# A graph attention kernel: in the last layer the row products are dealt to other engines

## The reference

```python
h = (x @ W.T).reshape(n, H, D)
alpha = einsum(h[src], a_src) + einsum(h[dst], a_dst)
enc = relu(edge_attr @ edge_W.T + edge_b).reshape(-1, H, D)
alpha = leaky_relu(alpha + sum(enc * h[dst], -1), 0.2)
ex = exp(alpha - segment_max(alpha, dst)[dst])
attn = ex / maximum(segment_sum(ex, dst)[dst], 1e-10)
out = segment_sum(h[src] * attn[..., None], dst) + bias
x = layernorm(x + out)
```

## Time and profile before

| | |
|---|---|
| median of 3 runs | 2146.94 us (2145.23 to 2147.84) |
| the profiled execution | 2150.75 us, span 2148.9 us, granted clock 0.844 |
| busy in the span | PE 1676.9 us (78%), DVE 1659.5 (77%), POOL 1552.5 (72%), ACT 1071.4 (50%) |
| row products on ACT, all layers (L1414) | 1840 instructions, 511.3 us |
| row products on POOL, the last layer (L1237) | 200 instructions, 129.0 us |

### The profile page before, as it was taken

How to read it: one execution, slowest core, us unless ns; L and a number is a source line. 1 busy time by engine, 2 the same in 40 slices (tenths; PEclk the granted TensorE clock), 3 DMA queues, 4 the chain that set the end, 5 groups by cost and what they waited for, 6 DMA issues and landing times. The chain is left out here.

```text
span 2148.9 us, 42137 instructions
## 1 busy us (share of the span) xinstructions
PE 1676.9 (78%) x9240; PEld 1039.6 (48%) x9240; DVE 1659.5 (77%) x4633; ACT 1071.4 (50%) x3670; POOL 1552.5 (72%) x1714
## 2 busy tenths in 40 slices
PE   7387888888885667778777776578999999899884
PEld 5244544544453434445444444345555555555551
DVE  5578877777779546666666667868999999999988
ACT  3134443443342435445455553546666666666655
POOL 3767777777777377777777776567778877778763
PEclk9578777877876868887888887879999999999985
DMA  6754444455640244444444641243444444444421
GB/s 195 178 144 134 140 139 137 138 140 155 185 124 29 89 127 136 135 135 134 134 130 135 198 121 37 91 124 106 130 135 132 127 125 129 132 130 134 133 67 60
DMA packets 131322, 274.32 MB, mean 128 GB/s; under 512 B 40389, under 2 KB 65968, under 8 KB 131061
## 3 DMA queue, kind: packets, MB, share of 16 engines
q0 software_dynamic: 64128, 181.33, 30.5%
q1 hardware_dynamic: 62259, 86.45, 13.4%
q10 hardware_dynamic: 4699, 3.86, 0.6%
HBM read 255.34 MB, written 17.20 MB: 127 GB/s over the span
## 5 line engine op out<-in xcount | busy, mean ns | idle before, releaser
L1225 POOL DMA_INDIRECT rows<-table,index_all x1320 | 1284.2, 973 | 481.1 <-issue 344.0
L1658 PE MATMUL bank<-rows,onehot 128*128 128x264 f32 (+1 forms) x2640 | 984.7, 483 | 178.1 <-ACT rows L1414 91.1
L826 DVE TENSOR_TENSOR sums<-sums,bank 128x264 f32 (+1 forms) x1320 | 552.7, 419 | 202.5 <-PE bank L1658 106.1
L1658 PEld LDWEIGHTS bank<-rows,onehot 128*128 128x128 f32 x2640 | 498.4, 224 | 386.7 <-ACT rows L1414 153.1
L1414 ACT ACTIVATE rows<-rows,wgt 128x33 f32<-128x33 f32 (+2 forms) x1840 | 511.3, 358 | 0.1
L1366 ACT CAST onehot<-bank 128x768 f32<-128x768 bf16 x240 | 177.7, 742 | 197.6 <-PE bank L1581 193.9
L1422 ACT ACTIVATE prod<-bank 128x512 f32<-128x512 f32 x240 | 134.8, 562 | 205.7 <-PE bank L1670 185.4
L815 DVE TENSOR_TENSOR rows<-rows,wgt 128x260 f32<-128x260 f32 (+2 forms) x480 | 216.0, 450 | 0.7 <-ACT wgt L1407 0.6
L1677 PE MATMUL bank<-late,onehotT 128*128 x1320 | 193.9, 283 | 0.7 <-DVE prod L835 0.7
L1373 ACT COPY scoreT<-bank 44x256 f32<-44x256 f32 (+2 forms) x120 | 39.5, 329 | 274.4 <-PE bank L1611 224.0
L835 DVE TENSOR_TENSOR prod<-prod,bank 128x512 f32<-128x512 f32 x240 | 151.8, 632 | 11.5 <-PE bank L1677 6.9
(11 more groups left out here) (200 smaller groups left out, 1787.6 us busy)
## 6 DMA issues: line engine op xcount, KB each, us to landing
locb<-loc_d SPq DMA_DIRECT2D x120, 352.0 KB, 3.8
rows<-table,index_all POOLq DMA_INDIRECT x1320
flags<-flags_d SPq DMA_DIRECT2D x520, 27.5 KB
table<-rows SPq DMA_DIRECT2D x25, 136.0 KB, 1.9
table<-rows SPq DMA_DIRECT2D x25, 134.0 KB, 3.0
late<-table SPq DMA_DIRECT2D x1, 3300.0 KB
table<-rows SPq DMA_DIRECT2D x25, 129.5 KB, 2.0
late<-table SPq DMA_DIRECT2D x1, 3212.5 KB, 14.8
```

Of the source, the lines that this page charges most:

```text
L826: done(v.tensor_tensor(a, a, sum_bank(l, t, s)[:, 0:VV], ALU.add), "add")
L1225: g.indirect_dma_start(out=rows[:, t.u, s, 0:ROW[l]], out_offset=None, in_=table[l], in_offset=bass.IndirectOffsetOnAxis(ap=index_all[:, t ...
L1658: done(m.matmul(sum_bank(l, t, s)[:, 0:VV], onehot[:, t.u, s, :], rows[:, t.u, s, 0:VV], start=True, stop=True), "agg")
```

## The change

One string: the word of the last layer in `OWNER`.

```diff
-OWNER = ("VAVVAVAVVVV", "VAAAAAAAAAA", "VVAVPAPPAPP")
+OWNER = ("VAVVAVAVVVV", "VAAAAAAAAAA", "VVVAPAPAPAP")
```

## The result

| | before | after |
|---|---|---|
| median, fastest to slowest | 2147.39 us (2145.23 to 2149.95, 4 runs) | 2176.78 us (2175.35 to 2177.55, 4 runs) |
| span of the profiled execution | 2148.9 us | 2175.2 us |
| DVE busy | 1659.5 us (77%) | 1652.9 us (76%) |
| ACT busy | 1071.4 us (50%) | 1124.5 us (52%) |
| POOL busy | 1552.5 us (72%) | 1533.2 us (70%) |

The kernel is slower by 29 us: ratio 1.0131, interval 1.0118 to 1.0145. The forecast was 2152, with a range to 2160. The direction was right and the size was not.

The account below looks back on a forecast made before the run. It took DVE alone to bound from row 4's add to the rescale, PE from there to row 4's add. 36 x (0.06 + 0.08) = +5.0 us on 2150.75 gave 2155.8; less 3.8 for the median, 2152, range 2149 to 2157.

Parts of the forecast that it names:

- two signs of being wrong: Row 4's product under 5.3 us after the rescale would mean faster; L717 waiting over 0.1 us would mean slower.
- The loop over row 0, row 2's load and row 4: Rescale, row 0's add, PE rows 2 to 4, row 4's add, DVE's own work: 17.00 us; change adds 0.06 a batch.
- The 0.58 us that DVE gains ahead of that wait: Dot product after row 0's add starts 0.58 us earlier; the gain ends at row 4's add, which waits for PE.
- DVE's product behind the rescale: Row 2's product, placed between rescale and row 0's add, takes 0.43 us against 0.71 for row 3's product now.
- The 11 us of this rule alone: VectorE and GpSimd exclusion alone would save 0.3 us a batch, 36 x -0.3 = -11 us, giving 2136.
- ACT's chain: On ACT, row 7's product, copy and exponentials precede step 6's encoding, whose end moves from 1723.74 to 1724.82.
- ACT becomes the pacemaker: Slower rival: ACT's chain 0.3 us longer than summed delays dot product and L717; +16 us, 2163; chance 0.08.
- PE's 1.06 us at row 8: PE's largest wait, for ACT at row 8, disappears; a rival had it on the path: -38 us, 2109, chance 0.02.
- Cost: +0.08 us a batch, with no slack behind it: DVE's dot product (L835) can start at 1724.86 instead of 1724.78, waiting for ACT's encoding; bounds 0 and +0.28.
- Row 7's add on DVE comes only behind the dot product of 1724.72, which takes 0.68, so the new wait is covered: PE's row 7 product comes about 0.6 us later, at 1724.4, but costs DVE nothing at row 7's add.
- From that add to the next rescale, 10.83 us, DVE stands for nobody else: From row 4's add to the rescale, DVE alone sets the pace, waiting for no other engine.
- The 0.06 of slots 2 and 3: Row 2's product behind the rescale delays row 0's add and row 4's add by 0.06 us a batch; bounds 0.00, +0.4.

Follow-up runs that it names:

- the best version: Kernel before with DVE on slots 0 and 2, ACT 1, 3, 5, 8, POOL the rest, register load at step 3: 2138.46 us against 2149.26, ratio 0.9949.

## Why the prediction was wrong in its size

The direction was right, for a reason that the forecast had: the encoding does come too late. But at a chance of 0.44 for slower against 0.41 for the same it was not sure of it, and five sixths of the loss come from something that its sum doesn't hold. Neither of its two signs of being wrong showed: row 4's product did not start earlier than 5.3 us after the rescale, and L717 did not wait.

Right, by its own steps:

- **The loop over row 0, row 2's load and row 4.** Row 0's add at +0.68 (forecast 0.68), row 2's load at +1.22 (1.23), row 4's product at +5.41 (5.42), the wait at row 4's add 0.49 (0.5). The 0.58 us that DVE gains ahead of that wait bought nothing. Slots 2 and 3 alone cost +2.8 us (0.6 to 4.9) where 2.2 were forecast.
- **DVE's product behind the rescale** took 0.42 us and not 0.71. The Trainium skill ("SBUF — State Buffer", Who interferes with whom) has VectorE and GpSimd shut each other out here; the trace agrees that the product is short once no product of POOL lies beside it (POOL's first one starts at 1712.13, and this product ended at 1711.28). The 11 us of this rule alone weren't gained, as the saving lies ahead of a wait.
- **ACT's chain.** Encoding at +9.42 and its end at +10.00, where the five steps summed to +9.44 and +10.04. The rival "ACT becomes the pacemaker", priced at 0.3 us more of chain, falls with this. Its 2163 was the nearest of the cases to the result, by luck: its chain isn't longer than summed.
- **PE's 1.06 us at row 8** are gone and bought nothing.

Wrong: the step "Cost: +0.08 us a batch, with no slack behind it", and the bounds on it, 0 and +0.28. The dot product is indeed 0.09 us late. But I priced a late instruction at its own lateness, and put the register load at nothing, without a word on it. The wait took something from the sequencer besides: its lead. What stood behind the dot product in DVE's order was not only row 7's add but also the load of 1.29 us, and all but 0.27 us of it (0.87 against the 0.60 without a load) had been hidden by that lead. The term is 0.09 + 0.73 = 0.82 us a batch where 0.06 + 0.08 = 0.14 was summed: 36 x 0.68 = 24.5 of the 25 us that the forecast of 2152 lacks. The same holds for "Row 7's add on DVE comes only behind the dot product of 1724.72, which takes 0.68, so the new wait is covered". It took row 7's add to be bound by the engine, when it was bound by the sequencer: it starts 0.3 us behind the load's end, before the change and after it.

Three signs were in the trace of before. Row 7's add had an idle time of 0.20 us put down to "issue", with no wait. The prediction passes over it with "From that add to the next rescale, 10.83 us, DVE stands for nobody else". It was the end of a load not wholly hidden. In the view of DVE's waits this add has 6.9 us in 31 pieces put down to "issue", more than the 4.6 us that the prediction calls DVE's only wait for another engine. And two batches, one of them shown above, already held the 1.60. From them the bound was to be had: 36 x (1.60 - 0.87 + 0.14) = 31 us, 2178.

How little slack there was: not the 0.98 us between the encoding's end and the dot product. Where the batches of one kernel differ (the one with slot 10 on ACT), encodings that end 0.03, 0.31 and 0.45 us ahead of the dot product's start have row 7's add 1.60, 1.32 and 1.18 behind that start: each time about 1.63 us from the encoding's end to the add. In the kernel before it was 0.98 + 0.87 = 1.85. So the true slack was 1.85 - 1.63 = 0.22 us. The load's rows agree: it starts 0.26 us behind the encoding's end before the change, and 0.05 after it. The change has the encoding end at +10.00 instead of +8.96 (1723.74 in the prediction's working), 1.04 later: 1.04 - 0.22 = 0.82 us, the batch's whole loss. The 0.06 of slots 2 and 3 isn't added to it but is in the 1.04, since ACT's chain begins behind row 4: with slot 7 alone the same batch is 17.78 us, 0.04 shorter than with the whole change.

What stays open is what limits the sequencer's lead (in the kernel before it reaches the load 0.72 us ahead of the dot product, while the engine is at row 6's add), why sort B is slow and turns the sign of slot 7, and what lowers the clock in the longer batches of the best version.

## What to carry to other kernels

## What the runs showed of the hardware that I had not expected

- A load of 11 registers from SBUF takes 1.29 us of DVE's sequencer (the median of 120 in the kernel before), and DVE's next add starts 0.3 us behind its end. Behind a dot product that had waited it made the add start 1.60 us after the dot product's start, against 0.60 without it: 1.00 us bare. The same 11 in two loads cost 0.75 us more. The Trainium skill ("DMA: Bandwidth & Descriptors", Latency and other measured facts) gives a floor of about 600 ns for such a load; the shortest one measured here, of 6 registers, took 0.81. It also states about 200 ns for each register ("Runtime: NRT & Kernel Launch", Instruction fetch mechanics). Worked out from that page, 11 registers would be 2.2 us, an estimate; for these from SBUF the trace has 1.29, and the measurement decides.
- The load did not start before the wait of the instruction ahead of it was over: in batches 0 to 36 of the two kernels it started at the earliest 0.046 us behind the encoding's end.
- Of six chips three run one and the same program at about 2150 us and three at about 2580, and an edit that costs 1.5% on the one sort gains 0.7% on the other.
